# Order of small stages in a two-layer graph network: adjacency blocks, root products, router and key/value products

## The chip, the cores and the metric

The kernel runs on one core of a Trainium2 chip. The metric is the device time of one execution in microseconds (us), as the median of several runs. The engines are called as in the profile: PE (TensorE, with its weight loads as PEld), DVE (VectorE), ACT (ScalarE), POOL (GpSimd) and SP (SyncE, which here only issues loads).

## The reference, cut to what matters

The input is x (625 nodes x 512 features), 10,000 edges (src, dst) and an edge type of 0 or 1. Everything is float32.

```python
xn = layernorm(x)
x = x + gnn0(xn, edges) + mix0(xn)
x = x + ffn0(layernorm(x))
xn = layernorm(x)
x = x + gnn1(xn, edges) + mix1(xn)
x = x + ffn1(layernorm(x))

# gnn0, two layers; h = relu(layer1(xn)), out = layer2(h)
w[r] = sum_b att[r, b] * basis[b]                 # 30 bases of 512 x 512, r = 0, 1
gate[r] = sigmoid(x @ gate_w[r])
agg = segment_sum(over edges of type r: gate[r] * x[col] @ w[r])
layer = agg + x @ root + bias
# mix0: kernel attention: kqv, exp features, y = qp (kp^T v) / D, proj, an MLP
# ffn0: 64 experts' router, top 2 of the softmax of x @ router_w, one shared FFN, gate, capacity 512
# gnn1: batchnorm, mean over neighbours @ W_conv, attention with 8 heads over the first
#       128 nodes by random features, batchnorm
# mix1: linear attention; ffn1: 8 experts, top 2, silu
```

## The kernel before, in words

One program for all engines, each with its own instruction stream; they meet through semaphores. The nodes lie in 5 tiles of 125 rows (`TT = 5`, `P = 125`), or as columns in 2 halves of 312 and 313 (`HALF`); features are 4 blocks of 128 (`KT = 4`). PSUM has 8 banks that are handed out in a ring by a list written out by hand, `PSUM_ORDER`: stage by stage, so many banks each. `claim` makes PE wait until the bank's last reader is done; PE counts each finished bank in the semaphore `psum_full`, for which `filled(stage, n)` gives the value, and ACT counts its reads in `act_read` (`ACT_READS` gives the order).

The stages in time, in the profiled execution:

- 13 to 84 us, the dense adjacency `AT` (two relations). For each of 5 blocks of destinations DVE writes one-hot rows from the edge lists (L986, L987), and PE multiplies them into four PSUM banks (L1396) in a hardware loop. Each bank is opened by a product with a row of zeros (L1387) and closed by another one 312 or 313 columns wide (L1400). After block 1 PE transposes all 5 tiles of h (the normalised input for mix0, 20 transposes, L1319), after block 2 those of xn.
- 84 to 272 us: mix0 and the neighbours' sums `Z1` = gated xn times `AT`. On POOL two transfers of 1,250 KB add bias rows into x (`x_bias`, L477), the second after the first has landed; then, on the same queue and as tiles of v come, 5 transfers `v_bias` add a bias to v. The product kptv on PE waits for all five.
- From 84 us on, DVE forms the weights `wrel` of both gnn layers out of 30 bases each: 2.35 us for one basis and relation (L1004), while SP loads the bases into a few slots of `weights` that it refills.
- 272 to 289 us: `h1T` = root1 times xn (L1505); to 323 us, the same banks get the products with `wrel` (L1511). Then ACT applies relu, PE computes the second layer's gates (40 products of 2 columns) and turns h1 into rows (20 transposes, L1333, bank stage `h1r`); ACT scales them by the gates.
- 334 to 377 us: `Z2`, the neighbours' sums of h1 (160 products); to 394 us `o2` = h1 times root2 (L1522, 40 products); to 422 us the `wrel` part of o2 (L1528), in which each float32 factor is split in a high and a low part, three products each. ACT makes the high parts (L719, L722), DVE the low ones (L1047, L1050). After Z2, POOL adds the two relations' adjacencies (L500, `A_sum`); DVE reduces the degrees (L1054) and scales to the mean (`A_mean`).
- 422 to 450 us: layernorm row by row (`layernorm_by_tile`: `make` a row, statistics, ACT's square root, `normalise`, one row behind), transposes `xfT`, router logits `rt`, the router on DVE (L1091 to L1112), the shared FFN, next layernorm, transposes `xn2` and, between them, 25 transposes of the adjacency (L1562, `adjacency_T`).
- 451 to 508 us: `aq`, `ak`, `av` (the 128 nodes' query, key, value), `uk` (random features of the keys; POOL squares aq and ak, L507 and L509, and reduces the maximum over partitions, L521), meanwhile batchnorm on DVE (`bn1`), split in halves (`xb_hi` on ACT, `xb_lo` on DVE, L1128), `xbw` (60 products), `uq`, `conv` (80 products), `kv` (16 small groups), `qfT` (16 transposes). When conv's last bank is read, DVE splits the result (L1151 to L1153) for `xk`, the next product.
- 508 to 842 us: the rest of attention, the second FFN's experts in a loop of PE products. The diff doesn't touch it.

Of the kernel before, what the change touches and what calls it, by code (L numbers as in the profile page):

```python
# [5 lines left out]
N = 625  # L6
H = 512
NE = 10000
P = 125
# [23 lines left out]
for _n, _c in COLS:  # L33
# [7 lines left out]
PSUM_ORDER = [("rng", 1), ("A0", 8), ("hT", 5), ("A2", 4), ("xnT", 5), ("A", 8),  # L41
# [28 lines left out]
A_BLOCK = [("A0", 0), ("A0", 4), ("A2", 0), ("A", 0), ("A", 4)]  # L70
# [5 lines left out]
XN2_TILE, ANT_TILE = (0, 2, 4, 6, 8), (1, 3, 5, 7, 9, 10, 11)  # L76
# [14 lines left out]
for _n, _c in PSUM_ORDER:  # L91
# [3 lines left out]
ACT_READS = [("A0", 8), ("hT", 5), ("A2", 4), ("xnT", 5), ("A", 8), ("kq", 16), ("v", 5), ("xdk", 1), ("wk", 5), ("ks", 1), ("kptvA", 1), ("xdq", 1), ("wq", 5),  # L95
# [10 lines left out]
def gps_two_layers(nc, I, out):  # L106
# [3 lines left out]
    with ctx:  # L110
# [71 lines left out]
        w2_hi = [t.rearrange("p (k n) -> p k n", k=KT) for t in (ew_hi[:, 1, :], ew_lo[:, 0, :])]  # L182
        w2_lo = [ew_hi[:, 2 + r, :].rearrange("p (k n) -> p k n", k=KT) for r in range(2)]

# [11 lines left out]
        root = [wmat(12288), wmat(4096)]  # L196
# [70 lines left out]
        sq_aq = slot[1][:, 1024:1536].rearrange("p (k t) -> p k t", k=KT)  # L267
        sq_ak = slot[1][:, 1536:2048].rearrange("p (k t) -> p k t", k=KT)
# [51 lines left out]

        for n in range(4):
            freed[TILE0["uk"] + n] = ("uk", 2 * n + 2)
            freed[TILE0["uq"] + n] = ("uq", 2 * n + 2)
# [10 lines left out]
        def filled(stage, count):  # L334

            return TILE0[stage] + count
# [104 lines left out]
        def _(pool):  # L441
# [37 lines left out]
            pool.wait_ge(S("xn_row"), 5)  # L479
            add_to(x, I["row_mlp_b2"].partition_broadcast(P).unsqueeze(1).to_broadcast([P, TT, H]), "x_bias")  # L480
# [18 lines left out]
            pool.wait_ge(S("psum_full"), filled("Z2", 16))  # L499
# [55 lines left out]
        def _(act):  # L555
# [27 lines left out]
            def transposed(stage, dst):  # L583

                for j in range(TT):
                    copy_out(stage, j, dst[:, :, P * j:P * j + P], B(stage, j)[:, 0:KT * P].rearrange("p (k t) -> p k t", k=KT))

# [28 lines left out]
            for j in range(TT):  # L616
                act.wait_ge(S("psum_full"), filled("hT", j + 1))
                for k in range(KT):
                    ins = act.activation(col(4)[:, k, P * j:P * j + P], B("hT", j)[:, P * k:P * k + P], ACT.Identity,
                                         scale=colvec("n1_g", k), bias=colvec("n1_b", k))  # L620
                ins.then_inc(S("act_read"), 1)
            adjacency_out(2)
            transposed("xnT", xnT)
            for j in range(3, TT):
                adjacency_out(j)
# [75 lines left out]
            for l, Z in enumerate(("Z1", "Z2")):  # L701
                if l == 1:
                    for n in range(8):
                        m, (a, w) = n // 2, HALF[n % 2]
                        copy_out("h1T", n, h1[:, m, a:a + w], B("h1T", n)[:, 0:w], ACT.Relu, bias=colvec("bias1", m))
                    load(root[1], I["L0_gnn_root2"].rearrange("(k p) n -> p k n", p=128), "root2_in")
# [5 lines left out]
                    for j in range(TT):  # L712
                        copy_out("h1r", j, row(GATED[1][1])[:, j, :], B("h1r", j)[0:P, :], ACT.Copy, scale=gates[:, 1, j, 1:2])
                for n in range(16):
                    r, m, (a, w) = n // 8, n // 2 % 4, HALF[n % 2]
                    copy_out(Z, n, col(Z_AT[r])[:, m, a:a + w], B(Z, n)[:, 0:w])
# [3 lines left out]
            for r in range(2):  # L720
                act.wait_ge(S("w_sum"), SUM_AT[1, NB - 1, r])
                act.activation(w2_hi[r], wrel[1][r], ACT.Copy).then_inc(S("o2_high"), 1)  # L722

            def columns_of(stage, n, j, dst):
                copy_out(stage, n, dst[:, :, P * j:P * j + P], B(stage, n)[:, 0:KT * P].rearrange("p (k t) -> p k t", k=KT))

            def adjacency_T(n):
                w = min(4, 25 - 4 * n) * P
                copy_out("xn2A", ANT_TILE[n], AT1[:, 500 * n:500 * n + w], B("xn2A", ANT_TILE[n])[0:P, 0:w])

            for j in range(TT + 1):
                if j < TT:
                    sqrt_of_tile("xf_row", 0, j)
                if j:
                    columns_of("xfT", j - 1, j - 1, col(2))
            act.wait_ge(S("gap"), 1)
            act.activation(rtp, rtp, ACT.Exp).then_inc(S("gap_exp"), 1)
            act.wait_ge(S("gap"), 2)
            act.activation(small[0:P, 30:35], small[0:P, 30:35], ACT.Exp).then_inc(S("gap_exp"), 1)
# [3 lines left out]
            for j in range(TT + 1):  # L743
                if j < TT:
                    sqrt_of_tile("xn2_row", 0, j)
                if j:
                    columns_of("xn2A", XN2_TILE[j - 1], j - 1, col(2))
                if 0 < j < TT:
                    adjacency_T(j - 1)
            for n in range(4, 7):  # L750
                adjacency_T(n)
# [1040 lines left out]
```

## Time and profile before

| | |
|---|---|
| median of 3 runs | 845.24 us (845.07 to 846.45) |
| the profiled execution | 843.48 us |
| its span, first to last instruction | 841.7 us |
| mean granted clock of TensorE | 0.974 of full |
| PE busy | 800.7 us (95%) |
| DVE busy | 539.5 us (64%) |
| ACT busy | 248.6 us (30%) |
| POOL busy | 148.2 us (18%) |

The span is what the trace covers; 1.8 us of the profiled execution lie outside it. Busy times of engines overlap, so they don't add up to the span. A row of a timeline gives start and duration, the engine, the line of the kernel, the operation, what is written and read, how many equal instructions the row takes together, and in brackets the idle time before it and the instruction that ended it.

### The profile page before, as it was taken

The numbers are of one execution on the slowest core, as the hardware profiler recorded it, in microseconds if no ns is written. First come the engines' busy times: TensorE is split into PE (matmuls) and PEld (weight loads), VectorE is DVE, ScalarE is ACT, GpSimd is POOL, SyncE is SP. The second block draws the span as 40 slices with busy tenths as digits, with TensorE's granted clock in tenths as the row PEclk, the third lists the DMA queues.
The fourth block names the chain that finished last, engine by engine and source line by source line (L and its number), as shares of the span: only waits on it lengthen the run. The fifth ranks groups of instructions, "written<-read, shape, count | busy, mean of one in ns | idle before, by whom it ended". The sixth has DMA issues, their size and how long they took to land.

```text
span 841.7 us, 10823 instructions
## 1 busy us (share of the span) xinstructions
PE 800.7 (95%) x3995; PEld 640.9 (76%) x3995; DVE 539.5 (64%) x743; ACT 248.6 (30%) x468; POOL 148.2 (18%) x96
## 2 busy tenths in 40 slices
PE   4999999999999999999998999997699999999997
PEld 3988766847477777765767778897598888888886
DVE  5876998979989999999777426068541111511112
ACT  4252223316411013222045332142432321432310
POOL 2011001120100000002201350031343330433300
PEclk9999999999999998999999999999589999999999
DMA  7533779796878768742041120000242120322001
GB/s 245 213 50 47 227 214 337 266 276 158 240 228 276 246 220 282 242 139 100 1 159 58 48 97 1 1 2 1 100 151 96 55 98 2 100 100 100 0 0 61
DMA packets 64211, 110.21 MB, mean 131 GB/s; under 512 B 6815, under 2 KB 16412, under 8 KB 64172
## 3 DMA queue, kind: packets, MB, share of 16 engines
q1 hardware_dynamic: 54476, 96.71, 34.5%
q0 software_dynamic: 6912, 7.70, 5.4%
q10 hardware_dynamic: 2784, 5.27, 1.7%
q8 instruction: 25, 0.41, 0.2%
q14 instruction: 14, 0.11, 0.0%
HBM read 105.81 MB, written 1.28 MB: 127 GB/s over the span
## 4 chain that ended last, share of the span: by engine, by line
PE 89%; DVE 6%; issue 2%; ACT 1%; POOL 1%; DVEq 0%; POOLq 0%
PE bank L1310 55%; PE bank L1730 13%; PE bank L1396 6%; PE bank L1511 4%; PE bank L1528 3%; PE bank L1522 2%; PE bank L1505 2%; PE bank L1326 1%; DVE st L890 1%; PE bank L1437 1%; PE bank L1333 1%; DVE slot L987 1%; ACT slot L581 1%; DVE slot L885 0%; DVE slot L1116 0%
## 5 line engine op out<-in xcount | busy, mean ns | idle before, releaser
L1004 DVE SCALAR_TENSOR_TENSOR weights<-weights,att 128x2048 f32<-128x2048 f32 x116 | 268.9, 2392 | 2.7 <-DMA weights<-in_L_gnn_basis 2.1
L1291 DVE CAST hid_hi<-slot 128x626 fp32r<-128x626 f32 x32 | 15.6, 487 | 160.7 <-ACT slot L846 160.7
L1310 PE MATMUL bank<-half,ew_hi 128*128 128x314 f32 (+1 forms) x512 | 114.0, 312 | 2.2 <-POOL ew_lo L550 2.2
L1310 PE MATMUL bank<-AT,slot 125*128 125x312 f32 (+1 forms) x400 | 105.9, 426 | 0.8 <-ACT slot L711 0.8
L1310 PEld LDWEIGHTS bank<-AT,slot 125*128 125x128 f32 x400 | 75.5, 189 | 31.0 <-ACT slot L711 1.0
L550 POOL TENSOR_TENSOR ew_lo<-weights,ew_hi 128x1024 fp32r<-128x1024 f32 x28 | 69.4, 2500 | 134.4 <-ACT ew_hi L828 134.4
L1310 PEld LDWEIGHTS bank<-half,ew_hi 128*128 128x128 f32 x512 | 88.4, 193 | 5.6 <-issue 2.9
L581 ACT ACTIVATE slot<-bank 128x312 f32<-128x312 f32 (+6 forms) x88 | 43.8, 525 | 148.7 <-PE bank L1310 128.9
L1310 PE MATMUL bank<-weights,slot 128*125 128x512 f32 (+5 forms) x306 | 86.9, 447 | 0.3 <-ACT slot L581 0.3
L846 ACT ACTIVATE slot<-bank,eb_now 128x312 f32<-128x312 f32 x64 | 33.3, 522 | 157.2 <-PE bank L1310 157.2
L1310 PE MATMUL bank<-half,ew_lo 128*128 128x312 f32 (+1 forms) x256 | 79.5, 310 | 0.0
L1310 PEld LDWEIGHTS bank<-weights,slot 128*125 128x125 f32 (+2 forms) x306 | 52.5, 205 | 30.1 <-issue 27.5
L1310 PE MATMUL bank<-slot,weights 128*128 128x313 f32 (+2 forms) x304 | 67.3, 381 | 0.1
L1730 PE MATMUL bank<-ew_lo,hid_hi 128*125 128x512 f32 x160 | 63.3, 396 | 0.0
L1730 PE MATMUL bank<-ew_hi,hid_lo 128*125 128x512 f32 x160 | 63.1, 395 | 0.0
L1730 PE MATMUL bank<-ew_hi,hid_hi 128*125 128x512 f32 x160 | 63.0, 394 | 0.0
L1310 PEld LDWEIGHTS bank<-slot,weights 128*128 128x128 f32 x304 | 50.4, 192 | 15.9 <-issue 1.2
L1396 PE MATMUL bank<-slot 125*125 125x312 f16 (+1 forms) x384 | 55.7, 306 | 3.9 <-DVE slot L987 3.8
L1396 PEld LDWEIGHTS bank<-slot 125*125 125x125 f16 x384 | 52.6, 141 | 6.8 <-DVE slot L987 5.6
L986 DVE TENSOR_SCALAR slot<-slot,small 125x625 f16<-125x625 f16 x96 | 40.5, 422 | 16.7 <-PE bank L1319 4.4
L1310 PEld LDWEIGHTS bank<-half,ew_lo 128*128 128x128 f32 x256 | 49.5, 193 | 0.0
L581 ACT ACTIVATE slot<-bank,cols 128x312 f32<-128x312 f32 (+1 forms) x42 | 21.7, 524 | 92.3 <-PE bank L1511 46.4
(297 smaller groups left out, 1116.4 us busy)
## 6 DMA issues: line engine op xcount, KB each, us to landing
weights<-in_L_gnn_basis SPq DMA_DIRECT2D x60, 1024.0 KB, 5.5
weights<-in_L_ffn_W SPq DMA_DIRECT2D x32, 512.0 KB, 4.5
weights<-in_L_mix_kqv_w SPq DMA_DIRECT2D x1, 3072.0 KB, 10.2
weights<-in_w_qkvT SPq DMA_DIRECT2D x3, 1024.0 KB, 5.4
slot<-slot POOLq DMA_DIRECT2D x10, 250.0 KB, 6.5
weights<-in_L_mix_mlp_w ACTq DMA_DIRECT2D x2, 1024.0 KB, 13.6
weights<-in_L_gnn_root ACTq DMA_DIRECT2D x2, 1024.0 KB, 8.7
slot<-in_row_mlp_b POOLq DMA_DIRECT2D x1, 1250.0 KB, 26.1
```

The costliest lines, as they stand in the source:

```text
L550: pool.tensor_tensor(ew_lo[:, c % 4, at:at + 1024], weights[:, 2048 * (c % 2) + at:2048 * (c % 2) + at + 1024], ew_hi[:, c % 4, at:at + 10 ...
L581: act.activation(dst, src, func, **kw).then_inc(S("act_read"), 1)
L846: act.activation(hid[:, f % 4, a:a + w], B("eh", n % 3)[:, 0:w], ACT.Silu, bias=eb1_now[:, f:f + 1]).then_inc(S("eh_out"), 1)
L986: dve.tensor_scalar(oh_src[j % 2][u], iota_src, small[0:P, bass.ds(EU * q0 + EU * i + u, 1)], None, ALU.is_equal)
L1004: ins = dve.scalar_tensor_tensor(wrel[layer][r], wmat(at), att[:, layer, r, b:b + 1], wrel[layer][r], ALU.mult, ALU.add)
L1310: ins = pe.matmul(out, a, b, start=i == 0, stop=i == len(pairs) - 1)
L1396: ins = pe.matmul(bkq[0:P, 0:w], oh_dst[j % 2][u][:, P * r:P * r + P], oh_src[j % 2][u][:, a:a + w], start=False, stop=False)
L1505: pe.matmul(bk[:, 0:w], root[0][:, k, 128 * m:128 * m + 128], xnT[:, k, a:a + w], start=k == 0, stop=False)
L1511: ins = pe.matmul(B("h1T", n)[:, 0:w], wrel[0][r][:, k, 128 * m:128 * m + 128], col(Z_AT[r])[:, k, a:a + w], start=False, stop=i == 2 * KT ...
L1522: pe.matmul(bk[0:P, :], h1[:, k, P * j:P * j + P], root[1][:, k, :], start=k == 0, stop=False)
L1528: ins = pe.matmul(B("o2", j)[0:P, :], t[r][:, k, P * j:P * j + P], wt[r][:, k, :], start=False, stop=r == 1 and k == KT - 1 and i == 2)
L1730: ins = pe.matmul(B("eb2", j)[0:P, :], a, b, start=f == 0 and i == 0, stop=f == 15 and i == 2)
```

## The change

- **Adjacency blocks**: the closing product is 1 column wide. h's and xn's transposes come in portions: 4 tiles of h after block 1, one of h and 3 of xn after block 2, 2 of xn after block 3. POOL's first `x_bias` transfer waits until the whole adjacency is in PSUM.
- **First layer's end**: h1T's banks are taken by halves of the nodes instead of by feature blocks (`by_half`), and the gates and transposes of tiles 0 and 1 are issued after 6 of the 8 groups of wrel products, those of tiles 2 to 4 after all.
- **Root products** of layer 2 come before Z2 instead of behind it. root2 is loaded, from ACT's queue, into the place of root1 as soon as PE has read that. Z2 uses three banks in turns; ACT's high parts of wrel come inside Z2.
- **xfT** transposes of tiles 0 to 3 lie among the last o2 products (tiles 0 to 2) and behind them; the rows are normalised at once rather than one row behind. The router takes the probabilities of the chosen experts in one product and divides the gate by the sum at the end: DVE operations L1095, L1101, L1103 to L1105 go, two new ones come; ACT's small exp goes.
- **xn2, aq, ak**: aq is computed after two tiles of xn2, the other three tiles' transposes follow it. The low half of each batchnorm block is formed between the scaling operations, and xbw waits block by block.
- **Adjacency transposes** are moved from between the xn2 tiles to after xbw; **kv** from after conv to before it.
- POOL's squares write to another buffer.

```diff
-PSUM_ORDER = [("rng", 1), ("A0", 8), ("hT", 5), ("A2", 4), ("xnT", 5), ("A", 8),
+PSUM_ORDER = [("rng", 1), ("A0", 8), ("hTa", 4), ("A2", 4), ("hTb", 1), ("xnTa", 3), ("A3", 4), ("xnTb", 2), ("A", 4),
...
-              ("m2", 5), ("Z1", 16), ("h1T", 8), ("gate2", 1), ("h1r", 5), ("Z2", 16), ("o2", 5),
+              ("m2", 5), ("Z1", 16), ("h1T", 8), ("gate2", 1), ("h1r", 5), ("Z2b", 3), ("o2", 5),
               ("xfT", 5), ("rt", 1), ("hf", 2), ("pos", 1), ("fy", 5),
-              ("xn2A", 12), ("aq", 1), ("ak", 1), ("av", 1), ("uk", 4), ("ad", 1), ("xbw", 5), ("uq", 4), ("conv", 8),
-              ("kv", 3), ("qfT", 4), ("xk", 5), ("at", 2), ("xv", 5), ("atT", 1), ("xkv", 1), ("ha", 1),
+              ("xn2a", 2), ("aq", 1), ("xn2b", 3), ("ak", 1), ("av", 1), ("uk", 4), ("ad", 1), ("xbw", 5), ("anT", 7), ("uq", 4), ("kv", 3), ("conv", 8),
+              ("qfT", 4), ("xk", 5), ("at", 2), ("xv", 5), ("atT", 1), ("xkv", 1), ("ha", 1),
...
+TURNS = {"o2": (0, 1, 2, 4, 6), "xfT": (3, 5, 7, 8, 9)}
...
-        root = [wmat(12288), wmat(4096)]
+        root = [wmat(12288), wmat(12288)]
...
@@ POOL
             pool.wait_ge(S("xn_row"), 5)
+            pool.wait_ge(S("psum_full"), filled("A", 4))
             add_to(x, I["row_mlp_b2"].partition_broadcast(P).unsqueeze(1).to_broadcast([P, TT, H]), "x_bias")
...
-            pool.wait_ge(S("psum_full"), filled("Z2", 16))
+            pool.wait_ge(S("psum_full"), filled("Z2b", 3))
             pool.tensor_tensor(AT0, AT0, AT1, ALU.add).then_inc(S("A_sum"), 1)
...
@@ ACT
+                    act.wait_ge(S("root1_used"), 1)
+                    load(root[1], I["L0_gnn_root2"].rearrange("(k p) n -> p k n", p=128), "root2_in")
                     for n in range(8):
-                        m, (a, w) = n // 2, HALF[n % 2]
+                        m, (a, w) = by_half(n)
                         copy_out("h1T", n, h1[:, m, a:a + w], B("h1T", n)[:, 0:w], ACT.Relu, bias=colvec("bias1", m))
-                    load(root[1], I["L0_gnn_root2"].rearrange("(k p) n -> p k n", p=128), "root2_in")
...
+                    if l == 1 and n in (11, 13):
+                        act.wait_ge(S("w_sum"), SUM_AT[1, NB - 1, (n - 11) // 2])
+                        act.activation(w2_hi[(n - 11) // 2], wrel[1][(n - 11) // 2], ACT.Copy).then_inc(S("o2_high"), 1)
...
@@ DVE
-                    if j:
+                    if at_once:
+                        normalise(j)
+                    elif j:
                         normalise(j - 1)
...
-            dve.tensor_tensor(b2, top2, top1, ALU.subtract).then_inc(S("gap"), 1)
...
-            dve.wait_ge(S("gap_exp"), 2)
-            link(dve.tensor_reduce(s1, T[1], AX.X, ALU.add))
+            dve.wait_ge(S("gap_exp"), 1)
+            dve.wait_ge(S("chosen"), 1)
+            dve.tensor_reduce(s1, T[1], AX.X, ALU.add)
+            link(dve.tensor_tensor(T[3], T[1], chosen, ALU.mult))
             link(dve.reciprocal(s1, s1))
-            link(dve.tensor_tensor(b2, b2, s1, ALU.mult))
-            dve.wait_ge(S("chosen"), 1)
-            dve.tensor_tensor(T[3], T[3], bc(s1, E0), ALU.mult)
-            link(dve.tensor_tensor(T[4], T[4], bc(b2, E0), ALU.mult))
-            link(dve.tensor_tensor(T[3], T[3], T[4], ALU.add))
...
             link(dve.tensor_reduce(gate, T[2], AX.X, ALU.add))
+            link(dve.tensor_tensor(gate, gate, s1, ALU.mult))
...
+            batchnorm(col(2), col(3), "g1", "bn1", "b1n", between=lambda k: lower_half(k - 1) if k else None)
+            lower_half(KT - 1)
...
@@ PE
-                    pe.matmul(bkq[0:P, 0:w], zero[:, 0:P], zero[:, 0:w], start=False, stop=True).then_inc(S("psum_full"), 1)
+                    pe.matmul(bkq[0:P, 0:1], zero[:, 0:P], zero[:, 0:1], start=False, stop=True).then_inc(S("psum_full"), 1)
                 if j == 1:
-                    to_cols("hT", row(3), "h_row")
+                    for i in range(4):
+                        tile_to_cols("hTa", i, i, row(3), "h_row")
                 if j == 2:
-                    to_cols("xnT", xn, "xn_row")
+                    tile_to_cols("hTb", 0, 4, row(3), "h_row")
+                    for i in range(3):
+                        tile_to_cols("xnTa", i, i, xn, "xn_row")
+                if j == 3:
+                    for i in range(2):
+                        tile_to_cols("xnTb", i, 3 + i, xn, "xn_row")
...
+            def second_gates(j0, j1):
+                bk = claim(pe, "gate2") if j0 == 0 else B("gate2")
+                pe.wait_ge(S("act_read"), READ0["h1T"] + (4 if j0 == 0 else 8))
+                for j in range(j0, j1):
+                    ins = group(bk[0:P, 2 * j:2 * j + 2], [(h1[:, k, P * j:P * j + P], gate_w[:, 1, k, :]) for k in range(KT)])
+                if j1 == TT:
+
+                    ins.then_inc(S("psum_full"), 3)
...
-            pe.wait_ge(S("act_read"), READ0["h1T"] + 8)
-            small_rows("gate2", h1, gate_w[:, 1, :, :], 2)
-            to_rows("h1r", h1)
-            neighbours("Z2")
+                if n == 5:
+                    second_gates(0, 2)
+                    h1_rows(0, 2)
+            second_gates(2, TT)
+            h1_rows(2, TT)
             pe.wait_ge(S("root2_in"), 16)
             for j in range(TT):
                 bk = claim(pe, "o2", j)
                 for k in range(KT):
                     pe.matmul(bk[0:P, :], h1[:, k, P * j:P * j + P], root[1][:, k, :], start=k == 0, stop=False)
+            neighbours("Z2")
...
+                        if j >= 2:
+                            tile_to_cols("xfT", j - 2, j - 2, row(1), "xf_row")
+            tile_to_cols("xfT", 3, 3, row(1), "xf_row")
...
-            for j in range(TT):
-                tile_to_cols("xn2A", XN2_TILE[j], j, row(1), "xn2_row")
-                if j < TT - 1:
-                    adjacency_T(j)
-            for n in range(4, 7):
-                adjacency_T(n)
-
-            pe.wait_ge(S("act_read"), READ0["xn2A"] + XN2_TILE[1] + 1)
+            for j in range(2):
+                tile_to_cols("xn2a", j, j, row(1), "xn2_row")
+            pe.wait_ge(S("act_read"), READ0["xn2a"] + 2)
...
+                if stage == "aq":
+                    for j in range(2, TT):
+                        tile_to_cols("xn2b", j - 2, j, row(1), "xn2_row")
...
-            pe.wait_ge(S("xb_low"), 4)
...
+                for k in range(KT):
+                    if j == 0:
+                        pe.wait_ge(S("xb_low"), k + 1)
...
+            pe.wait_ge(S("A_mean"), 5)
+            for n in range(7):
+                adjacency_T(n)
             random_features("uq", aqT)
-            pe.wait_ge(S("act_read"), READ0["xbw"] + 5)
+            key_values()
+            pe.wait_ge(S("act_read"), READ0["anT"] + 7)
```

`by_half(n)` is an existing function that gives feature block n % 4 and node half n // 4. In `tile_to_cols` 4 transposes fill one bank.

## Rows read from the trace of the kernel before

**Rows 1.** Chain of waits: shares by engine, then four pieces of it in order of time.

```profile
PE 89%; DVE 6%; issue 2%; ACT 1%; POOL 1%; DVEq 0%; POOLq 0%
...
43.84 1.28 DVE slot L987
...
69.92 1.33 DVE slot L987
...
83.43 0.67 PE bank L1400 x4
...
153.59 0.54 PE bank L1437 x2
```

**Rows 2.** Timeline of DVE, 38 to 46 us (start, duration, instruction, idle time before).

```profile
42.02 0.38 DVE L986 TENSOR_SCALAR slot<-slot,small 125x625 f16<-125x625 f16 x1
42.31 1.44 DVE L987 TENSOR_SCALAR slot<-slot,small 125x250 f16<-125x250 f16 x1
```

**Rows 3.** Timeline of PE, 38 to 78 us, equal instructions taken together.

```profile
54.08 0.74 PE L1387 MATMUL bank<-zero 1*125 1x312 f16 x4 [0.40 <-ACT slot L619]
...
76.81 1.41 PE L1396 MATMUL bank<-slot 125*125 125x312 f16 x9 [0.36 <-DVE slot L987]
```

**Rows 4.** Line L477, POOL's accumulating transfers: issue in ns, first and last start.

```profile
L477 POOL DMA_DIRECT2D slot<-in_row_v_b x5: 847/847/913, 122.3 to 136.0; - x5
...
L477 POOL DMA_DIRECT2D slot<-in_row_mlp_b x1: 3351/3351/3351, 41.7 to 41.7; - x1
```

**Rows 5.** DMA issues: count, KB each, median us from issue to landing.

```profile
slot<-in_row_mlp_b POOLq DMA_DIRECT2D x1, 1250.0 KB, 26.1
...
slot<-in_row_v_b POOLq DMA_DIRECT2D x5, 250.0 KB, 6.8
```

**Rows 6.** Windows: busy PE, PEld, DVE, ACT, POOL; PEclk, DMA share, GB/s.

```profile
126.00:154.00 28.00, 28.00 (x118) 20.62 (x116) 24.10 (x14) 9.54 (x12) 3.14 (x4) 1.00 1.06 345
170.00:172.00 2.00, 2.00 (x3) 0.94 (x4) 1.93 (x3) 0.00 (x0) 0.10 (x1) 0.50 0.57 116
...
328.00:333.50 5.50, 5.50 (x27) 5.46 (x26) 5.50 (x4) 2.80 (x5) 0.00 (x0) 0.50 0.99 310
```

**Rows 7.** Timeline of PE, 322 to 342 us.

```profile
323.60 5.69 PE L1310 MATMUL bank<-gate_w,slot 128*125 128x2 f32 x40 [0.61 <-ACT slot L581]
329.15 4.58 PE L1333 MATMUL bank<-ident,slot 128*125 128x128 f32 x20
334.50 7.89 PE L1310 MATMUL bank<-AT,slot 125*128 125x312 f32 x29 [0.78 <-ACT slot L711]
```

**Rows 8.** Timeline of all engines, 372 to 396 us.

```profile
376.94 5.72 POOL L500 TENSOR_TENSOR AT<-AT 125x3125 f32<-125x3125 f32 x1 [144.74 <-PE bank L1310]
...
393.78 2.38 PEld L1528 LDWEIGHTS bank<-ew_hi,half 128*125 128x125 f32 x11 [0.59 <-DVE ew_hi L1050]
```

**Rows 9.** Line L1004, DVE's sums of the bases: ns, least, median, most.

```profile
L1004 DVE SCALAR_TENSOR_TENSOR weights<-weights,att x116: 2341/2345/7764, 86.5 to 384.9; 128x2048 f32<-128x2048 f32 x116
```

**Rows 10.** Timeline of DVE, 421 to 442 us.

```profile
435.25 0.49 DVE L1103 TENSOR_TENSOR slot<-slot,small 125x320 f32<-125x320 f32 x1
...
437.75 0.75 DVE L1116 SCALAR_TENSOR_TENSOR slot<-bank,small,slot 125x512 f32<-125x512 f32 x1
```

**Rows 11.** Timeline of PE, 446 to 510 us.

```profile
448.50 0.62 PE L1326 MATMUL bank<-ident,slot 125*128 125x125 f32 x4 [1.18 <-DVE slot L885]
...
450.80 7.31 PE L1310 MATMUL bank<-slot,weights 128*128 128x128 f32 x64
...
502.60 3.68 PE L1310 MATMUL bank<-slot 128*128 128x65 f32 x32
506.12 1.92 PE L1626 MATMUL bank<-ident,slot 128*128 128x128 f32 x16
```

**Rows 12.** Timeline of DVE, 448 to 510 us.

```profile
469.02 1.84 DVE L1137 SCALAR_TENSOR_TENSOR small<-small 128x8 f32<-128x8 f32 x1 [3.10 <-POOL small L521]
...
504.56 2.76 DVE L1153 TENSOR_TENSOR hid_lo<-slot,hid_hi 128x2500 fp32r<-128x2500 f32 x1
```

More of the change, by code:

```diff
@@ L319, in gps_two_layers @@
                 freed[TILE0[name] + n] = (name, n + 1)
+        for n in range(3):
+            freed[TILE0["Z2b"] + n] = ("Z2", 16)
         for n in range(4):
@@ L334, in filled @@
         def filled(stage, count):
+            if stage in TURNS:
+                return TILE0["o2"] + TURNS[stage][count - 1] + 1
             return TILE0[stage] + count
@@ L734, in _ @@
                 if j:
-                    columns_of("xfT", j - 1, j - 1, col(2))
+                    columns("xfT", j - 1, j - 1, col(2))
             act.wait_ge(S("gap"), 1)
             act.activation(rtp, rtp, ACT.Exp).then_inc(S("gap_exp"), 1)
-            act.wait_ge(S("gap"), 2)
-            act.activation(small[0:P, 30:35], small[0:P, 30:35], ACT.Exp).then_inc(S("gap_exp"), 1)
             for n in range(2):
@@ L767, in _ @@
                 copy_out("xbw", j, xbw[:, j, :], B("xbw", j)[0:P, :])
+            for n in range(7):
+                adjacency_T(n)
+            for n in range(3):
+                w = min(6, 16 - 6 * n)
+                copy_out("kv", n, kv_sb[:, 6 * n:6 * n + w, :], B("kv", n)[:, 0:65 * w].rearrange("p (g d) -> p g d", g=w))
             act.wait_ge(S("phi_bias"), 2)
@@ L920, in batchnorm @@
                     ins.then_inc(S(name), 1)
+                    if between:
+                        between(k)
             def bc(v, e):
@@ L1327, in tile_to_cols, with cols_out @@
                 ins.then_inc(S("psum_full"), 1)
-            def to_rows(stage, src):
-                for j in range(TT):
-                    bk = claim(pe, stage, j)
-                    for k in range(KT):
-                        ins = pe.transpose(bk[0:P, 128 * k:128 * k + 128], src[:, k, P * j:P * j + P], ident[:, :])
-                    ins.then_inc(S("psum_full"), 1)
-            def cols_out(stage, w, at, act_in, tiles=KT, n0=0, k_in=KT, columns=None):
+            def cols_out(stage, w, at, act_in, tiles=KT, n0=0, k_in=KT):
                 for m in range(tiles):
@@ L1538, in _ @@
             pe.wait_ge(S("ffn_in"), 48)
-            for j in range(TT):
-                tile_to_cols("xfT", j, j, row(1), "xf_row")
-                if j == 1:
-                    claim(pe, "rt")
-                if j:
-                    router_logits(j - 1)
+            claim(pe, "rt")
+            for j in range(TT - 1):
+                router_logits(j)
+            tile_to_cols("xfT", 4, 4, row(1), "xf_row")
             router_logits(TT - 1).then_inc(S("psum_full"), 1)
@@ L1558, in adjacency_T @@
             def adjacency_T(n):
[L1559 removed]
+                bk = claim(pe, "anT", n)
                 for b in range(4 * n, min(4 * n + 4, 25)):
@@ L1579, in _ @@
                 ins.then_inc(S("psum_full"), 1)
+                if stage == "aq":
+                    for j in range(2, TT):
+                        tile_to_cols("xn2b", j - 2, j, row(1), "xn2_row")
             bk = claim(pe, "av")
@@ L1583, in _, with key_values @@
             pe.wait_ge(S("projT_in"), 32)
+            def key_values():
+                pe.wait_ge(S("phi"), 1)
+                pe.wait_ge(S("act_read"), READ0["av"] + 1)
+                for g in range(16):
+                    if g % 6 == 0:
+                        bk = claim(pe, "kv", g // 6)
+                    h, c = g // 2, g % 2
+                    ins = group(bk[:, 65 * (g % 6):65 * (g % 6) + 65], [(ke[:, h, 128 * c:128 * c + 128], v_aug[:, h, :])])
+                    if g % 6 == 5 or g == 15:
+                        ins.then_inc(S("psum_full"), 1)
             def random_features(stage, t):
```

168 lines of the change are left out of this document (87 added, 81 removed), and 3 rows, old and new, of the table ACT_READS.

## The prediction

> **What bounds the kernel now.** I read the chain of waits first. PE is 89% of it and DVE 6% [rows 1], so only what PE executes, or what it waits for, moves the end. Then I went through PE's timeline for its idle times and the instruction that ended each, and looked at the engine named in its own timeline. The expert loop after 600 us and all from 508 us on is the same in both kernels, so the question is how far the start of xk moves.
>
> Four places come out. In the adjacency stage the chain passes twice through a slow one-hot of DVE, 1.28 and 1.33 us [rows 1]; the ops beside it take 0.38 us, and the slow one starts at 42.31 and takes 1.44 [rows 2]. POOL's first x_bias issue runs from 41.7 for 3.35 us [rows 4]: the slow ops lie inside it, and the second pair lies the same way at the second issue. Further on, PE waits 0.61 us for ACT ahead of the gates and 0.78 ahead of Z2 [rows 7]; the transposes between cost 4.58 us at a granted clock of 0.50, which is the 1.2 GHz level, from about 326 to 333.5 [rows 6, 7]. Near 450 PE idles 1.18 us per xn2 tile behind DVE's normalising [rows 11]. And DVE's split of conv (ends 504.56 + 2.76 = 507.32) is hidden, barely, by kv and qfT on PE from 502.60 to 508.0 [rows 11, 12].
>
> **The change, part by part** (negative is time saved)
>
> *Adjacency, 38 to 84 us.* With x_bias held back until A is complete, the two slow pairs go: -2.6 (1.28 + 1.33). The PSUM wait of 0.40 ahead of block 2's opening goes, since ACT then owes 4 tiles rather than 5; and the 0.36 wait at 76.81 is covered by the 8 transposes now put there [rows 3]: together -0.7. The transposes keep their number, so they only move. The four closing products take 0.67 us on the chain [rows 1] at 312 columns. One column can't cost less than nothing (saving 0.67) and, by the pace of 2-column products (5.69 us for 40, slow clock included, so at most 0.14 each and 0.57 for four [rows 7]), saves at least 0.1. I take 0.33 per block, between the two, since these weights load one row only, and count four blocks, as the first block's closing lies beside DVE's start of its next loop: -1.3. Sum -4.6 (-3.7 to -6.0). PE and DVE's sums of bases both start at A's end, so both shift alike.
>
> *x_bias beside mix0.* A ends at 83.43 + 0.67 = 84.1 [rows 1], now about 79.5, and the first transfer is issued then instead of at 41.7 [rows 4]. Its landing took 26.1 us [rows 5], so 105.6; the second (27.1 in the same view) lands near 133. The v_bias issues behind it on the same queue came between 122.3 and 136.0 and landed 6.8 us later [rows 4, 5], the last one at 143. kptv needs them all at 153.6 [rows 1], now 149. So there are 6 us to spare against equal speeds, and I cost this at 0. But the transfer now shares with the bases' loads: the DMA share is already 1.06 between 126 and 154 [rows 6]. If that doubled the second landing it would land near 160, and PE would stall up to 18 us. Both ends are kept. The 60 loads of bases are on another queue; DVE's sums run back to back with a median of 2,345 ns and a least of 2,341 [rows 9], so some later landings are absorbed by the slots loaded ahead, and 6% of the chain is all that DVE has [rows 1].
>
> The Trainium skill ("SBUF — State Buffer", box "The 'DVE blocks DMA' trap (SWDGE)") states that a transfer issued by POOL can't write its descriptors while DVE holds the port pair that both share. It speaks against issuing x_bias under DVE's sums. Here five v_bias issues under those sums took 847 ns at the median and least [rows 4] and the sums kept their 2,345 ns, so this case's trace shows no such loss under L1004; by the rule each of two issues would wait for at most one sum, which the spare 6 us hold too.
>
> *Gates, rows of h1, root products.* The root products (17.2 us) now stand between the rows and Z2, so ACT's gating is covered: -0.75 of the 0.78. The 0.61 ahead of the last gates stays. root2 is asked for at 289 instead of 323, for use after 333: no wait. Splitting 40 gates and 20 transposes into 16 + 8 inside the dense products and 24 + 12 after them may spare the fall of the clock. The row from 328 to 333.5 has 5.5 us at half the clock, of which half, 2.75, would be lost if all of it scales; the transposes alone show 4.58 - 20 x 0.12 = 2.2 against the pace of qfT's 16 in 1.92 us [rows 7, 11]. The fall began after 326, so with that piece it costs 3.8 at most. Against that, the fall at 170 came after a shorter stretch of small products and went on into wide ones (0.50 at 170 to 172 [rows 6]); a fall after the second burst would cost the first root products as much. Between 0 and -3.8 I take -1.5, as for one fall in place of the long one. Z2 in three banks: a group of 10 products takes 2.7 us (7.89 for 29 [rows 7]) and ACT, 30% busy over the span, has one bank to copy per group and two groups of slack for its high parts: 0, and up to 2.7 if one of them outlasts the slack. POOL's addition (5.72 us [rows 8]) lay on a sum of DVE that took 7.76 us instead of 2.35 [rows 9], and the low part L1050 came only just before o2 [rows 8]. Now the sums end some 5 us before Z2 does, and the addition moves to 393, where it lies on a low part wanted only half way through the o2 products: 0.
>
> *xfT, router.* Two transposed tiles stand in the o2 products and the logits follow at once; T4 is then the last: the router gets its input 0.1 earlier besides the 0.75. DVE loses three operations on 320 elements, 0.49 us each like L1103, and two on 5 elements, and gains one of 0.49 and a small one [rows 10]: two times 0.49 and one small op, 1.1 in all. The first fy bank, which L1116 at 437.75 also reads, is full only some 0.75 sooner: -0.75. Together -0.85.
>
> *xn2, aq, batchnorm, xbw.* aq is half of 7.31 us [rows 11] and now lies in the idle times between tiles: -3.65. The 9 last adjacency transposes ahead of aq go, -1.0 at qfT's pace, while ak waits for ACT's copies of the last tiles, +0.8. So -3.85 up to xbw, if batchnorm follows: it starts as early, its square root no longer stands behind aq's copy, and the low halves are interleaved. The 25 adjacency transposes after xbw are 25 x 0.12 = +3.1. The keys' exponentials hang on POOL's maximum and a DVE op that took 1.84 us beside POOL's cast [rows 12]; xbw's fourth tile wants one of their banks, and xbw starts 4 us earlier while the maximum does so only in part: +1.5 (0 to 4).
>
> *kv before conv.* kv's 3.6 us only change place. But DVE's split ends 4.7 us after conv's end (507.32 - 502.60), and only qfT's 1.9 [rows 11, 12] is left to cover it: +2.9. The bounds are 2.5 and 3.3.
>
> **Sum:** -4.6 + 0 - 0.75 - 1.5 - 0.85 - 3.85 + 3.1 + 1.5 + 2.9 = -4.05, on the profiled execution 843.48 - 4.05 = 839.4. The median of the runs shown is 1.76 above that execution, so 841.2.
>
> **Rivals.** (a) *The x_bias queue stalls PE: slower.* v_bias stands behind x_bias on POOL's queue. For it: the DMA share of 1.06 in the window [rows 6], where x_bias did not lie before. Against: the v_bias transfers issued inside this same window landed in 6.8 us each [rows 5], a fifth of x_bias's bytes in a quarter of its time, so the sharing costs them little, and there are 6 us of slack. It decides once the last v_bias lands 4 us after 149, at 153. With the second landing 20 us later than I take, at 153, and v_bias 4 us behind, PE stalls 8: 841.2 + 8 = 849. (b) *DVE's small ops under POOL's squares: no change.* The squares of aq now fall on batchnorm's small operations. A DVE op of 8 columns took 1.84 us beside POOL [rows 12]. One such hit of 1 us and a wait of 3 for the exponentials (+1.5 over my value) give -4.05 + 2.5, which is 843.7; two hits and the full wait of 4 give -4.05 + 2 + 2.5, which is 845.7. From one hit on the case is no longer told from no change. (c) *The clock doesn't fall at all: faster still.* Then the 3.8 are won rather than 1.5: 838.9. For it: the first burst is short; against: the row at 170.
>
> **How the numbers follow.** Forecast as worked out (839.5 to 843.4) 0.47; (c) and better 0.17; (b) 0.20; (a) 0.16. A measurement of this kernel tells 0.2%, or 1.7 us, from no change. Faster is the forecast and (c), less a little of the edge: 0.62. Same is most of (b): 0.21. Slower is (a) and the edge of (b): 0.17. The range leaves out the stall beyond 6 us and the last bit of (c): 837 to 848; the likeliest case alone has 839.5 to 843.4.
>
> **What the profile after would show.** No one-hot over 1 us; A's end near 79.5; x_bias issued there, landings of 26 to 40 us; no idle time of PE ahead of L1437 (if there is, rival a). PEclk around 325 to 335: one short fall or none. Z2 without idle, o2 near 387. Idle PE of about 2.9 us ahead of xk, ended by DVE's low half, and 1 to 2 us inside xbw, ended by ACT. If the wait ahead of xk is absent, or xbw starts less than 3 us earlier relative to the router's end, the respective step is wrong.

## The result, and the profile after

The changed kernel takes 869.25 us (865.5 to 873.48, 4 runs) against 845.4; the ratio is 1.0297, 95% interval 1.0266 to 1.0328. It is slower by 3%, where 841.2 and a range of 837 to 848 had been forecast. The profiled execution is the longest of the four, with a span of 871.7 us against 841.7, 30 us more.

The chain of waits of the changed kernel, shares by engine and line, and pieces of it in order of time (start, duration, what):

```profile
PE 84%; DVE 5%; issue 5%; DMA 4%; POOL 1%; ACT 1%; DVEq 0%; POOLq 0%
...
78.02 0.33 PE bank L1409 x4
...
94.46 21.05 DMA weights<-in_L_gnn_basis
...
120.18 16.32 DMA weights<-in_L_gnn_basis
...
138.88 1.38 DVE slot L1039
...
154.56 14.02 issue
168.57 0.56 PE bank L1452 x2
```

PE's share fell from 89% [rows 1] to 84, and there is a share for DMA, which there was none of before. The adjacency now ends at 78.35 (78.02 + 0.33) instead of 84.1. The kptv products begin at 168.57 instead of 153.59. PE's timeline, 136 to 230 us:

```profile
141.25 1.98 PE L1337 MATMUL bank<-eps,slot 128*125 128x1 f32 x10 [3.26 <-DVE slot L1040]
...
168.57 0.56 PE L1452 MATMUL bank<-ones,slot 125*128 125x1 f32 x2 [14.02 <-issue]
168.99 1.20 PE L1453 MATMUL bank<-slot 125*128 125x256 f32 x2
```

The view names no releaser for the 14.02 us; by the code PE there waits for a transfer, `v_bias`, and the landing below fits. The 3.26 us are a wait for a small sum of squares on DVE, which stands in DVE's queue behind sums that wait for bases. The transfers of the changed kernel (count, KB, median us from issue to landing):

```profile
weights<-in_L_mix_mlp_w ACTq DMA_DIRECT2D x2, 1024.0 KB, 30.1
...
slot<-in_row_mlp_b POOLq DMA_DIRECT2D x1, 1250.0 KB, 36.2
slot<-in_row_bias POOLq DMA_DIRECT2D x1, 1250.0 KB, 40.2
slot<-in_row_v_b POOLq DMA_DIRECT2D x5, 250.0 KB, 14.7
```

Against [rows 5], x_bias lands 10 and 13 us later after its issue, v_bias twice as late at the median. The first three of its five took 12 to 15 us although the second x_bias was still in flight. The last two were issued at 126.8 and 130.3, close to ACT's issues of the 3 MB of weights for proj and the MLP (129.4 to 130.6), and took 32.9 and 38.2 us. The last one so landed at 168.5, when PE goes on. The waits of DVE, in total, times, longest:

```profile
DVE weights L1032 <- DMA weights<-in_L_gnn_basis: 25.2, 8, 5.9
```

Then the clock. Windows of the changed kernel (busy times of PE, PEld, DVE, ACT, POOL, then PEclk, DMA share, GB/s):

```profile
141.00:149.00 8.00, 7.75 (x26) 6.59 (x27) 4.29 (x3) 5.57 (x8) 0.00 (x0) 0.57 1.06 310
126.00:154.00 28.00, 24.74 (x97) 19.60 (x96) 19.13 (x10) 8.90 (x11) 1.70 (x2) 0.88 1.07 293
154.00:168.50 14.50, 0.56 (x3) 0.15 (x1) 7.92 (x5) 0.00 (x0) 0.00 (x0) 0.66 0.76 226
168.50:182.00 13.50, 13.43 (x44) 11.65 (x44) 13.50 (x7) 0.36 (x2) 0.00 (x0) 0.50 0.59 213
182.00:195.00 13.00, 11.93 (x56) 10.34 (x57) 1.30 (x1) 4.46 (x13) 3.79 (x5) 0.72 0.44 104
```

During the wait the granted clock falls to the 1.2 GHz level and stays there over the kptv products and behind them. A pair of them takes 1.06 us on the chain where it took 0.54 [rows 1]. It also falls behind the shorter wait of 3.26 us (0.57 from 141 to 149): the 50 products that follow take 3.4 us longer than before the change.

The ledger of the adjacency's end to h1T's start: 188.5 us before (84.1 to 272.5), 223.0 after (78.3 to 301.3), +34.5. The two waits are 17.3 of it. The kptv products take 13.1 us instead of 6.4 (+6.7), the piece up to the next wait for ACT 9.2 instead of 5.4 (+3.8), gates and transposes ahead of the MLP 8.7 instead of 6.4 (+2.2). The stretch before kptv is 3.5 longer without its wait, nearly all of it the fall of the clock just named, and Z1's is 1.0 longer. That makes 34.5. The 2.2 and the 1.0 don't come from the stall. The clock was back at full from 200 to 216. The fall after that costs 5.1 us, as the sum of (1 - PEclk) over windows of 1 us, against 1.7 before the change. In the first two experiments below it is 5.1 in the changed kernel without the stall, and 1.7 in the kernel before with the stall. Against the 34.5 stand the 5.7 us of the adjacency; the rest of the kernel is +1.2 in all.

### The profile page after: what moved, and what is told of

Same layout as the page of the kernel before. It is cut to its first block, busy times and chain, and to the rows that moved or that the text cites. A ratio compares the mean times of both kernels' runs of the same rounds, so it can differ in the third digit from the quotient of the medians.

```text
span 871.7 us, 10820 instructions
## 1 busy us (share of the span) xinstructions
PE 816.9 (94%) x3995; PEld 653.6 (75%) x3995; DVE 537.8 (62%) x740; ACT 248.6 (29%) x467; POOL 147.5 (17%) x96
## 4 chain that ended last, share of the span: by engine, by line
PE 84%; DVE 5%; issue 5%; DMA 4%; POOL 1%; ACT 1%; DVEq 0%; POOLq 0%
PE bank L1337 48%; PE bank L1779 13%; PE bank L1405 6%; DMA weights<-in_L_gnn_basis 4%; PE bank L1551 4%; PE bank L1570 3%; PE bank L1563 2%; PE bank L1544 2%; PE bank L1344 2%; PE bank L1658 2%; PE bank L1453 1%; DVE weights L1032 1%; PE bank L1536 0%; ACT slot L595 0%; DVE tmp L928 0%
## 5 line engine op out<-in xcount | busy, mean ns | idle before, releaser
L1032 DVE SCALAR_TENSOR_TENSOR weights<-weights,att 128x2048 f32<-128x2048 f32 x116 | 264.0, 2345 | 25.9 <-DMA weights<-in_L_gnn_basis 25.2
L1337 PE MATMUL bank<-weights,slot 128*125 128x512 f32 (+5 forms) x306 | 89.3, 457 | 0.7 <-ACT slot L750 0.7
L595 ACT ACTIVATE slot<-bank 125x512 f32<-125x512 f32 (+7 forms) x62 | 31.2, 538 | 106.8 <-PE bank L1337 96.9
L1014 DVE TENSOR_SCALAR slot<-slot,small 125x625 f16<-125x625 f16 x96 | 36.7, 382 | 14.7 <-PE bank L1405 5.8
## 6 DMA issues: line engine op xcount, KB each, us to landing
slot<-in_row_mlp_b POOLq DMA_DIRECT2D x1, 1250.0 KB, 36.2
```

The lines of the kernel that those rows point to most:

```text
L595: act.activation(dst, src, func, **kw).then_inc(S("act_read"), 1)
L1014: dve.tensor_scalar(oh_src[j % 2][u], iota_src, small[0:P, bass.ds(EU * q0 + EU * i + u, 1)], None, ALU.is_equal)
L1032: ins = dve.scalar_tensor_tensor(wrel[layer][r], wmat(at), att[:, layer, r, b:b + 1], wrel[layer][r], ALU.mult, ALU.add)
L1337: ins = pe.matmul(out, a, b, start=i == 0, stop=i == len(pairs) - 1)
```

## The experiments

### Which part costs

One line of the change undone:

```diff
             pool.wait_ge(S("xn_row"), 5)
-            pool.wait_ge(S("psum_full"), filled("A", 4))
             add_to(x, I["row_mlp_b2"].partition_broadcast(P).unsqueeze(1).to_broadcast([P, TT, H]), "x_bias")
```

> The changed kernel without POOL's wait for the whole adjacency ahead of the first x_bias transfer; all else stays. Theory A (x_bias beside the loads of bases and MLP weights is the whole loss): x_bias is issued near 42 again, both transfers land before the bases' loads start in earnest, PE has no long wait ahead of the kptv products (L1452), DVE waits under 4 us for bases. The slow one-hots return (+2.6), so the adjacency gains about 3 us instead of 5.7; with -1.0 (h1T to o2) and +0.5 (o2 to xk) as in the trace of the changed kernel that gives 842 us (840 to 844). Theory B (the reordering itself costs a large part, by the root weights' load or the new order): it stays above 855 us.

Measured: 840.0 us (838.03 to 846.44, 10 runs), ratio to before 0.9963 (0.9938 to 0.9987); PE has no wait ahead of the kptv products. The same line added to the kernel before (there with 8 banks):

> The kernel before with only that wait added. Theory A: the fast one-hots (-2.6) and then x_bias landings of 35 to 45 us, base loads landing in over 15 us, PE waiting 10 to 20 us for v_bias, and half the clock after it: 865 to 873 us. Theory B: under 855 us.

Measured: 867.79 us (866.48 to 872.45), ratio 1.03 (1.0257 to 1.0343); PE waits 15.5 us ahead of the kptv products, x_bias lands after 36.0 and 39.4 us. So theory A holds both ways: this one wait makes +29 us in the changed kernel and +23 in the kernel before (both net of what the adjacency gains by it), and the rest of the change makes it faster by 4.7 (1 to 5 by the interval). Why the two figures differ by 6 is not resolved.

### Why the transfer is so slow: the number of rows

```diff
-            add_to(x, I["row_mlp_b2"].partition_broadcast(P).unsqueeze(1).to_broadcast([P, TT, H]), "x_bias")
-            pool.wait_ge(S("x_bias"), 16)
+            for a, n in ROW_PARTS:
+                add_to(x[a:a + n], I["row_mlp_b2"].partition_broadcast(n).unsqueeze(1).to_broadcast([n, TT, H]), "x_bias")
+            pool.wait_ge(S("x_bias"), 32)
...
-            pool.wait_ge(S("x_bias"), 32)
+            pool.wait_ge(S("x_bias"), 64)
```

The row_bias2 transfer is split in the same way; `ROW_PARTS` is ((0, 112), (112, 13)).

> The changed kernel, wait kept, with each x_bias transfer issued as two, rows 0 to 111 and rows 112 to 124. Theory A1 (a transfer of 125 rows is served by few of the 16 DMA engines, for which the bases' loads must queue; flat DMA share of 0.31 while it is alone): the 112 rows are served by all engines, each pair lands in about 8 to 13 us at a DMA share near 1, the v_bias transfers land in under 20 us and PE's wait ahead of L1452 falls below 5 us: 838 to 848 us. Theory A2 (the volume of the transfers or their packets' overhead is what costs, however it is spread): landings stay over 25 us and the time over 860 us.

Measured: 837.83 us (836.74 to 838.46), ratio 0.9922 (0.9891 to 0.9953). With the wait still there, the 29 us are gone and PE has no wait ahead of the kptv products. The landings of this run:

```profile
slot<-in_row_v_b POOLq DMA_DIRECT2D x5, 250.0 KB, 7.2
...
slot<-in_row_mlp_b POOLq DMA_DIRECT2D x1, 1120.0 KB, 14.9
slot<-in_row_bias POOLq DMA_DIRECT2D x1, 1120.0 KB, 14.4
```

With no wait for the adjacency and the same split:

> Both: no wait for the adjacency, and x_bias in 112 + 13 rows. Both landings are done by about 65 us. Four issues rather than two lie on DVE's one-hots: by theory A1 the second issue comes near 52 rather than 68, in the same stage, with the same slow pairs: within 1.5 us of the variant with the wait taken away and unsplit transfers, 842 us. Theory A2: the same, since the landings are hidden either way.

Measured: 834.05 us (833.6 to 835.37), ratio 0.988 (0.9849 to 0.991). That is 6 us under the unsplit variant, where no more than 1.5 was expected: the slow one-hots went too (the adjacency ends 4.6 us sooner). In this run, and in the kernel before, the first x_bias transfer is nearly alone on the DMA engines. This run, 40 to 53 us (busy tenths in 40 slices, packets, and the queue's share of 16 engines):

```profile
DMA  0000000005699999999999999995999956510000
...
DMA packets 673, 1.29 MB, mean 99 GB/s; under 512 B 47, under 2 KB 47, under 8 KB 672
...
q0 software_dynamic: 672, 1.28, 65.0%
```

The kernel before, 40 to 68 us:

```profile
DMA  0000000045644333333333333333333333433310
...
DMA packets 2018, 1.32 MB, mean 47 GB/s; under 512 B 1391, under 2 KB 1391, under 8 KB 2016
...
q0 software_dynamic: 2016, 1.29, 28.8%
```

Engine time is share x 16 x window: 0.65 x 16 x 13 = 135 us, against 0.288 x 16 x 28 = 129. The same bytes take nearly the same engine time, but 125 rows are served at a flat three tenths, which is about 5 of 16 engines, for some 17 us after a busier start, and 112 rows by nearly all for 7. The 125-row form also has three times the packets; its engine time is no larger, so the spread and not the packets is what differs. The Trainium skill ("DMA: Bandwidth & Descriptors", section "Why a DMA increments its semaphore by 16 and not by 1") states that a transfer is dealt to the largest number of engines up to 16 that divides the slowest dimension of both its sides; for 125 rows that is 5, for 112 rows 16. This case's traces agree (the queue's share from 42 to 68 us is 31.0%, and 0.31 x 16 = 5.0; for 112 rows it is 103% from 43 to 50). The same section names an exception, by which some copies issued by POOL use 16 engines at other row counts too; the 125-row transfers here show nothing of it.

Base loads issued between 79 and 95 us took 16 us at the median in the changed kernel, and up to 33.6 further on, where those of the kernel before took 5 to 10. The likely reason is that a load of a basis is spread over more engines, lands when the slowest of those has done its part, and so waits for the few that x_bias holds. No view here shows single engines, so this last step is argued; that the delay goes when x_bias is spread is measured.

POOL's one issue of 3.35 us becomes two of 1.6 to 1.7 that start 1.2 us apart, and the one-hots beside them slow down to 0.58 us (0.74 beside the second transfer) instead of 1.44:

```profile
41.32 0.58 DVE L1016 TENSOR_SCALAR slot<-slot,small 125x250 f16<-125x250 f16 x1
41.52 0.55 DVE L1015 TENSOR_SCALAR slot<-slot,small 125x625 f16<-125x625 f16 x1
41.99 0.57 DVE L1016 TENSOR_SCALAR slot<-slot,small 125x250 f16<-125x250 f16 x1
42.18 0.54 DVE L1015 TENSOR_SCALAR slot<-slot,small 125x625 f16<-125x625 f16 x1
```

The split alone, in the kernel before:

> The kernel before, with nothing changed but the two x_bias transfers in 112 + 13 rows. The slow one-hots of 1.25 to 1.47 us become ones of about 0.55 as in the early split variant, so the adjacency ends 3 to 4 us sooner: 840.5 to 842 us. If the slow ones in the kernel before were hidden by something, 844 us.

Measured: 839.17 us (838.53 to 842.37, 10 runs), ratio 0.9951 (0.9931 to 0.9971): 4.6 us faster; the adjacency's last closing product starts at 78.7 instead of 83.8. The gain is a little more than expected.

### Which of the two transfers

The wait ahead of the second transfer instead of the first:

```diff
             pool.wait_ge(S("x_bias"), 16)
+            pool.wait_ge(S("psum_full"), filled("A", 4))
             add_to(x, I["row_bias2"].partition_broadcast(P).unsqueeze(1).to_broadcast([P, TT, H]), "x_bias")
```

> The changed kernel with the wait for the adjacency ahead of the second x_bias transfer instead of the first, whole 125-row transfers. It asks which of the two costs. If the loss comes from where a transfer on few DMA engines meets a full load queue (from about 110 us on, when MLP and projection weights are asked for besides the bases, the DMA share is over 0.9 without a gap), the first transfer's place beside bases alone costs little and the second one's much: here the second one is issued at 80 and landed near 116, ahead of v_bias, so 842 to 847 us. If each transfer beside the bases costs its share of the loss alike, half of some 29 us remains: 852 to 858 us.

Measured: 840.75 us (836.62 to 844.76, 8 runs), ratio 0.9956, a little below the 842 to 847 of the first case. The second transfer lands after 38.3 us, DVE waits 8.8 us for bases, yet v_bias lands in 7.1 and PE isn't late. One long transfer beside the bases is absorbed. And the first transfer held, the second one issued behind the proj_bias ones:

> The changed kernel with POOL's wait for the adjacency kept and whole 125-row transfers, but the second x_bias transfer issued after the proj_bias ones. It takes the second transfer out of the stretch with v_bias and the MLP weights. Theory A (the second transfer, landed at 156, is what v_bias and the bases' loads collide with): PE's wait of 14 us ahead of the kptv products goes, v_bias lands within 10 us, 840 to 846 us. Theory B (the first transfer alone, issued at 79, puts the loads so far behind that they don't recover): over 855 us. Should x_y come late for ACT's second set of gated rows, 1 to 8 us on top of theory A.

Measured: 847.4 us (842.56 to 851.25, 10 runs), ratio 1.0031. The wait ahead of kptv goes as theory A said, but the loss doesn't all go. PE now waits further down, before the `wrel` part of the o2 products. The wait, the DVE operation that ends it and POOL's addition of the adjacencies:

```profile
PE bank L1570 <- DVE ew_hi L1079: 8.6, 1, 8.6
...
L1079 DVE TENSOR_TENSOR ew_hi<-weights,ew_hi x2: 2280/5042/7805, 386.9 to 394.6; 128x2048 fp32r<-128x2048 f32 x2
...
386.21 6.32 POOL L514 TENSOR_TENSOR AT<-AT 125x3125 f32<-125x3125 f32 x1 [149.20 <-PE bank L1337]
```

DVE's sums waited 15.9 us for bases (10.7 in five pieces and 5.2 ahead of their first operation), and that came out at the end of their queue, where the split halves stand. That is only part of the 8.6 us: the late low half now lies beside POOL's addition and takes 7.8 us instead of 2.3, which is 5.5 of them. The changed kernel's own low halves took 2.3, since there POOL's addition came after them.

So PE's stall ahead of kptv takes both transfers in a row. In each of these two runs one long transfer lies beside the bases and has landed by 120 us, when the v_bias issues begin, and v_bias lands in 7.1 us. In the changed kernel the delay of DVE (25.2 us) is not seen at o2; PE itself was 27.7 us late there.

### The reordered parts

Based on the variant with early, split x_bias (834.05 us). kv put back behind conv:

```diff
             random_features("uq", aqT)
-            key_values()
...
+            key_values()
             pe.wait_ge(S("phi"), 2)
```

(with its places in the bank list, in ACT's order of reads and in ACT's copies moved alike)

> The variant with early x_bias in 112 + 13 rows (834.0 us), with the kv products put back behind conv. Theory A (the 2.9 us that PE waits for DVE's low half ahead of xk are the price of kv before conv): that wait goes, 831 us (830.5 to 832). Theory B (kv before conv covers another wait, such as that for the copies of the adjacency's transposes or the queries' exponentials, which then comes back ahead of conv): 833.5 to 835 us.

Measured: 831.02 us (830.71 to 836.58), ratio 0.9856 (0.9815 to 0.9896), the fastest of all, as theory A said. The wait is in the changed kernel's PE timeline, 500 to 540 us, and not in this run's:

```profile
531.52 1.91 PE L1675 MATMUL bank<-ident,slot 128*128 128x128 f32 x16
536.30 0.49 PE L1337 MATMUL bank<-ew_hi,hid_hi 128*125 128x512 f32 x1 [2.87 <-DVE hid_lo L1180]
```

```profile
493.41 1.92 PE L1676 MATMUL bank<-ident,slot 128*128 128x128 f32 x16
495.08 0.47 PE L1338 MATMUL bank<-ew_hi,hid_hi 128*125 128x512 f32 x1
```

The clock falls behind this wait too: 1.7 us of (1 - PEclk) within some 5 us of xk's start, in all eight traces with kv before conv, and in none of the five with kv behind it.

Root products behind Z2 again:

```diff
+            neighbours("Z2")
             pe.wait_ge(S("root2_in"), 16)
             for j in range(TT):
...
-            neighbours("Z2")
```

> The same variant with layer 2's root products issued after Z2, as before the change, while the bank list, the three banks of Z2 and the place of root2 stay. Theory A (root first covers ACT's gating of the rows and nothing else): PE waits 0.8 us for ACT ahead of Z2, 834.8 us. Theory B (root first also gives DVE and ACT time for the split halves): PE also waits for a low half ahead of the o2 products, 0.5 to 3 us more, 835.5 to 838 us. With the transposes of h1 directly ahead of Z2's 312-column products the granted clock may fall for 3.4 us, which costs 1.7 more.

Measured: 842.2 us (840.52 to 844.72, 10 runs), 8 more than 834.05; neither theory had that. PE waits for ACT ahead of Z2, much longer than the 0.78 of [rows 7]:

```profile
327.59 6.69 PE L1338 MATMUL bank<-AT,slot 125*128 125x312 f32 x14 [3.89 <-ACT slot L733]
```

The change has ACT scale each tile's rows by both gates in turn, where it did the first relation's five tiles first; Z2 begins with the first relation and needs all five of those. The four operations in between make about 2.3 of the 3.9 us (an estimate from ACT's starts, 0.57 us apart); the rest is that fewer transposes are left to cover ACT. The clock is then low from about 322 to 334, where the base variant has no fall, and Z2's products take 45.1 us instead of 42.3. Wait and slower products are 6.7 us; the spans of the two profiled executions differ by 5.1 (838.7 against 833.6), since this one was 1.2 ahead before that stage. That the medians differ by 8 is not resolved further.

Closing products wide again, on the variant with kv behind conv:

> The variant with early x_bias in 112 + 13 rows and kv behind conv (831.0 us), with the adjacency's closing products 312 and 313 columns wide again. The traces show 0.32 us for four narrow ones and 0.67 for four wide ones. If they lie on the chain in all blocks, 0.35 x 4 to 5 = +1.4 to +1.8 us: 832.4 to 832.8. If DVE's restart hides them in most blocks, under +0.5.

Measured: 835.66 us (833.25 to 838.77) against 831.02. The adjacency's last closing starts 1.6 us later (79.1 against 77.5), as expected. The other 3 us are not the closers' work: the profiled runs lose 20.5 and 17.1 us to the clock (one minus PEclk, summed over windows of 1 us from 80 to 640 us). v_bias and proj_bias in 112 + 13 rows too:

> The same variant with the v_bias and proj_bias transfers in 112 + 13 rows too. If these landings (6.7 and 9.8 us) are hidden, no change: 833.5 to 834.5 us. If ones of five engines still delay the loads beside them or PE's proj stage, up to 2 us faster; if ten more issues on POOL's queue, 0.85 us each, delay what stands behind them (x_y needs proj_out), up to 2 us slower.

Measured: 839.03 us (833.62 to 839.31) against 834.05, which is beyond the 2 us expected at most. Its landings were hidden already and it gains nothing; whether the ten more issues cost or only the clock's falls differ (18.8 us lost against 17.1, the adjacency's last closing starts at 78.8 against 77.8) stays open.

## Why the prediction was wrong, step by step

The step that failed is "x_bias beside mix0", costed at 0. It took the first landing as 26.1 us again, the second as 27.1, and gave v_bias 6 us of slack. The landings were 36.2 and 40.2, the second one ended at 155.8 instead of 133, and v_bias, issued behind it and beside the MLP's weights, at 168.5. Rival (a) named this mechanism and gave it 0.16, but priced it at 8 us. The step itself had written that a doubled landing could stall PE by up to 18 us and that both ends were kept, yet the range stopped at a stall of 6. Its slack of 6 us was wrong the other way: it moved kptv forward by the adjacency's gain but not the v_bias issues, which came at 117.3 to 130.3. With both moved the slack is 10.5, and the stall came all the same.

Three things were missing from the rival's price. The stall itself was 14.0 us. The bases' loads were put behind, which the step took to be absorbed by the slots loaded ahead: DVE waited 25.2 us, and since two small sums for PE stand in the same queue, PE waited 3.3 too. And the clock fell behind both waits: 3.4 us of the ledger are slow products behind the short one, 10.5 (6.7 + 3.8) behind the long one. POOL's wait for the adjacency, measured by taking it away, is worth 29 us.

What could have been read from the trace of before: the three tenths at which the DMA engines stood for some 17 of the 26 us of a landing. x_bias was not slow there for want of free engines; it used few of them. The argument against the rival, that v_bias landed in 6.8 us within the busy window, compared a transfer of 250 KB with one of 1,250 that holds its engines about four times as long (26.1 us against 6.8). The rule of the Trainium skill on descriptors ("SBUF — State Buffer", box "The 'DVE blocks DMA' trap (SWDGE)") was weighed and let go, and the trace after bears that out: the first issue took 4.19 us instead of 3.35, the second 3.05 as before. The first v_bias issue took 2.33 instead of 0.91, but it began while that of x_bias still ran.

The other steps, after against before:

- Adjacency, -4.6: measured -5.7. The wait's part is -4.3 by the variant without it (82.4 against 78.1), where 2.6 had been taken: each collision slows three or four one-hots, of which the chain shows one. The rest is -1.4 instead of -2.0. The four narrow closings take 0.33 us against 0.67, as taken.
- Gates, h1 rows, root first, -0.75 and -1.5 for the clock: -1.0 in all from h1T's start to that of o2's `wrel` part. The 0.78 goes; the clock's fall is there as before (356 to 364, 3.4 us lost). In the variants with the changed order and split transfers it is one fall of half that length (1.7 us lost) or none. Two traces with the new order and whole transfers show half a fall or none as well. The bounds 0 and -3.8 held; the value -1.5 had nothing to fix it, and the changed kernel's own trace gives 0.
- xfT and rt, -0.1: -0.6. Router to xbw, -0.75 and -3.85: -4.6 (30.8 us against 35.4), right.
- Exponentials inside xbw, +1.5: 0. xbw takes 14.0 us as before. Adjacency transposes +3.1: +2.7. kv before conv, +2.9: +2.9 in the trace and 3.0 by the experiment. The 1.7 us by which the unchanged part from xk on got longer is the fall of the clock behind that wait, which the term left out.
- Rival (b) did not come: no wait inside xbw, and o2 to xk is +0.5 where my terms made +2.8. Rival (c), no fall there at all, is seen in the variant with early split transfers and in the one with kv behind conv.

Without the wait on the adjacency the kernel measures -4.7 (840.0 against 844.66). That this is near the forecast sum of -4.05 is luck: the sum has -2.6 for the slow one-hots, which that variant still has, so the terms left make -1.45. Its profiled execution is one of the two longest of its ten (846.33) and doesn't show where the difference comes from. The variant with the wait kept and x_bias in 112 + 13 rows has all the terms; it measures -6.8 (837.83).

## What to carry to other kernels

Before a transfer is moved beside others, read from its quiet stretch how many DMA engines it holds (share x 16), not only how long it takes: here a landing of 26 us at a share of 0.31 became 36 to 40 us beside the bases' loads, and those took 16 us at the median and up to 34 instead of 5 to 10. Give transfers a row count that all 16 engines can share, and send the remainder by itself (here 112 + 13 rows). And add the slow products behind a stall of PE to its price: here 1.7 us behind a wait of 2.9, 3.4 behind one of 3.3, and 10.5 behind one of 14.0.

## What the runs showed that was not expected

The granted clock falls in pieces that cost about 1.7 us each or a multiple of it, at places that differ between variants of the same work: 17.1 to 25.6 us lost from 80 to 640 us in the traces without a long stall. Variants that differ by a microsecond of work can so differ by five; verdicts of 1 to 4 us between them need more runs than these had. The split of x_bias was meant for its landing and gave 4.6 us in the kernel before, with one-hots of 0.58 to 0.74 us instead of 1.44 beside POOL's issues. Whether that comes from the spread, the shorter single issues or from having a third of the packets was not separated.
